# First attention batch from unsplit float32 operands, and new call orders on all five queues

## What is computed

```python
q  = (layernorm(x) @ w_q)           # 16 heads of 64, w_q 256 x 1024
kv = context @ w_kv                 # context 8 x 120 x 256, w_kv 256 x 2048
x  = x + tanh(g0) * (softmax(q k / 8) v @ w_out + b_out)
z  = layernorm(x)
gate = top-2 of softmax(z @ Wr.T), renormalised      # 8 experts
x  = x + tanh(g1) * sum_e gate_e * (silu(z @ W1_e.T) @ W2_e.T)   # DFF 1024
```

## Time and profile before

| what | us |
|---|---|
| median of 3 runs | 570.75 |
| lowest and highest of the 3 | 564.15, 574.33 |
| the profiled execution | 573.52 |
| its span in the profile | 571.5 |

### The profile page before, as it was taken

One profiled execution on the slowest core, in us unless ns is written; L12 is line 12 of the kernel. 1 busy time (PEld: TensorE's weight loads), 2 busy tenths in 40 slices (PEclk: granted clock), 3 DMA queues, 4 the chain that ended last, 5 costly groups with the idle time before them and its releaser, 6 DMA issues.

```text
span 571.5 us, 17675 instructions
## 1 busy us (share of the span) xinstructions
PE 484.5 (85%) x6526; PEld 428.0 (75%) x6527; DVE 361.5 (63%) x855; ACT 370.4 (65%) x576; POOL 365.6 (64%) x372
## 2 busy tenths in 40 slices
PE   0268799999999999997969799893999999999990
PEld 0156668888888888884859688783898898988980
DVE  4988897988988888989845456431343434444430
ACT  1877999998989898998533655351555555555540
POOL 0796977798989898999984372224355455444531
PEclk9998999999999999999776989996999999999996
DMA  8921514262725344342298569664678776878421
GB/s 275 395 81 51 191 59 165 74 223 39 248 52 177 114 131 147 111 161 47 95 136 326 136 98 292 196 199 108 197 213 240 222 239 199 255 206 261 111 32 16
DMA packets 34846, 93.13 MB, mean 163 GB/s; under 512 B 4967, under 2 KB 24565, under 8 KB 27490
## 3 DMA queue, kind: packets, MB, share of 16 engines
q1 hardware_dynamic: 25634, 81.86, 44.8%
q0 software_dynamic: 8576, 10.30, 9.6%
q10 hardware_dynamic: 576, 0.14, 0.1%
HBM read 74.17 MB, written 18.12 MB: 161 GB/s over the span
## 4 chain that ended last, share of the span: by engine, by line
DMA 36%; PE 20%; POOL 15%; issue 10%; DVE 10%; ACT 6%; POOLq 0%; SPq 0%; ACTq 0%; DVEq 0%
DMA out<-yt,row_of 34%; PE j_bank L1719 6%; POOL stage L632 5%; PE j_bank L1614 4%; POOL pT L587 4%; POOL stage L634 2%; ACT pT L834 2%; PE st_bank L1794 2%; ACT pT L833 2%; DMA w2s<-in_ctxT 2%; POOL w2s L636 2%; PE o_bank L1614 2%; PE j_bank L1681 2%; PE max_pair L1773 1%; PE st_bank L1614 1%
## 5 line engine op out<-in xcount | busy, mean ns | idle before, releaser
L681 POOL DMA_INDIRECT out<-yt,row_of x39 | 65.8, 1688 | 121.8 <-DMA out<-yt,row_of 108.0
L1614 PE MATMUL st_bank<-xsT,w_tile 128*128 128x128 f16 x1872 | 115.8, 223 | 4.0 <-issue 3.7
L1614 PEld LDWEIGHTS st_bank<-xsT,w_tile 128*128 128x128 f16 x1872 | 111.2, 100 | 6.3 <-issue 5.0
L1453 DVE SCALAR_TENSOR_TENSOR hT<-hf,h_scale,hT 128x512 f16<-128x512 f32 x78 | 58.3, 751 | 90.5 <-ACT hT L961 90.4
L1614 PE MATMUL o_bank<-w2s,hT 128*128 x936 | 110.2, 275 | 1.5 <-DVE yt L1462 0.8
L1614 PEld LDWEIGHTS o_bank<-w2s,hT 128*128 128x128 f16 x936 | 90.6, 99 | 12.6 <-issue 2.0
L955 ACT ACTIVATE hf<-st_bank,z_scale 128x512 f32<-128x512 f32 x78 | 52.9, 678 | 45.3 <-PE st_bank L1614 43.0
L587 POOL TENSOR_TENSOR pT<-pT 120x512 f16<-120x512 f32 x64 | 76.3, 1206 | 4.4 <-ACT pT L834 4.2
L961 ACT ACTIVATE hT<-hf,h_scale 128x512 f16<-128x512 f32 x78 | 56.3, 722 | 14.3 <-PE o_bank L1614 5.8
L833 ACT ACTIVATE pT<-st_bank,exp_bias,logit_scale 120x512 f32<-120x512 f32 x64 | 50.0, 781 | 12.8 <-PE st_bank L1797 9.2
L632 POOL TENSOR_SCALAR stage<-stage,upw 128x512 f32<-128x512 f32 x32 | 54.0, 1688 | 5.1 <-ACT w_hi L928 4.7
(11 more groups left out here) (208 smaller groups left out, 908.4 us busy)
## 6 DMA issues: line engine op xcount, KB each, us to landing
w_tile<-w_split SPq DMA_DIRECT2D x39, 1024.0 KB, 5.2
stage<-in_w SPq DMA_DIRECT2D x16, 1024.0 KB, 5.2
w_split<-w_hi SPq DMA_DIRECT2D x8, 512.0 KB, 2.9
w_split<-stage SPq DMA_DIRECT2D x8, 512.0 KB, 4.0
out<-x SPq DMA_DIRECT2D x17, 128.0 KB
w2s<-in_wkv SPq DMA_DIRECT2D x2, 1024.0 KB, 10.2
xin<-in_x SPq DMA_DIRECT2D x8, 256.0 KB, 3.2
xres<-in_x SPq DMA_DIRECT2D x16, 128.0 KB
```

Source lines behind the costliest of these rows:

```text
L681: pool.indirect_dma_start(out=out[0:rows], out_offset=bass.IndirectOffsetOnAxis(row_of[:, t:t + 1], 0), in_=yt[t % XG][:], in_offset=None, ...
L1453: nc.vector.scalar_tensor_tensor(out=hT[par][:, 1, 4 * a:4 * a + 4, :], in0=hf[par][:, 512 * a:512 * a + 512].rearrange("p (c n) -> p c n" ...
L1614: ins = pe.matmul(out, lhs[i](a), rhs[i](c), start=(i == 0 and a + c == 0), stop=(i == n - 1 and a == 1))
```

## The change

1. Batch 0's keys, queries and values are computed from unsplit float32 operands, in one plain float32 matmul per pair of blocks instead of three float16 ones. The scale factors are multiplied into the other operand (`first_context` on DVE, twice; `x_low(0)`), so the results come out in the same scale. `x_high(0)` goes. The float32 copies lie in `xn2` and `xn2T`, unused at that time.
2. The context's piece for batch 0 goes. The splits of the weights are moved behind batch 0's products in the call orders, and on POOL and in `split_high` they wait until these products are done. `SUMS` changes from (2, 4) to (1, 3).
3. SP loads x of batch 0 first, then w_q, context, w_k, w_v, four x tiles, w_out, and then x of batch 1 (which waits for `x_T(0)`) ahead of the stage loads.
4. New call orders on all five queues and in the four job lists. No instruction is added or removed by this part. In them, on PE, `tile_T(0)`, `tile_T(1)` and three up halves stand ahead of `values(7, 3, 0)`; before it was `tile_T(0)` and one up half. On DVE `tile_experts(4, 0)` stands right behind `norm2_rows(5)`; before it was behind `route(5)` and more. On POOL `gather(5)` stands ahead of `norm2_factors(7)`; before it was behind it. `gather(13)` stands behind `add(8)` in both.

```diff
-SUMS = (2, 4,)
+SUMS = (1, 3,)
-PIECES = (((0, M), (M, B * M)), ((0, INNER // 2), (INNER // 2, INNER)), ...
+PIECES = (((M, B * M),), ((0, INNER // 2), (INNER // 2, INNER)), ...
...
+            sp.dma_start(xin[:], x_b[0]).then_inc(xin_in, 16)
+            sp.dma_start(raw_q, wq).then_inc(raw_in[2], 16)
+            sp.dma_start(raw_ctx, ctxT).then_inc(raw_in[0], 16)
+            sp.dma_start(raw_k, wkv[:, :, 0:INNER]).then_inc(raw_in[1], 16)
+            sp.dma_start(raw_v, wkv[:, :, INNER:2 * INNER]).then_inc(raw_in[3], 16)
...
+            load_x(1)
...
                 pool.wait_ge(w_high[i][j], 1)
+                for name in {1: ("K" + "ab"[j],), 2: (f"Q{2 * j}", f"Q{2 * j + 1}"), 3: ("V" + "ab"[j],)}.get(i, ()):
+                    pool.wait_ge(job_full, JOBS.fulled(name, 0))
...
+            def first_context(b, i):
+                if b:
+                    return
+                w = (1, 3)[i]
+                dve.wait_ge(up_done[0], 1)
+                dve.wait_ge(up_done[w], 1 + (i > 0))
+                nc.vector.tensor_scalar(ctx32[i], raw_ctx[:, :, 0:M], up[:, 0:1], up[:, w:w + 1], ALU.mult,
+                                        ALU.mult).then_inc(ctx32_done, 1)
...
+                if b == 0:
+                    src = bank_full("XT", b)
+                    dve.wait_ge(up_done[2], 1)
+                    nc.vector.tensor_scalar(xnT32, src[:], up[:, 2:3], None, ALU.mult).then_inc(job_free, 1)
+                    return
...
+            def plain(out, lhs, rhs):
+                for i in range(len(lhs)):
+                    ins = pe.matmul(out, lhs[i], rhs[i], start=(i == 0), stop=(i == len(lhs) - 1))
+                return ins
...
+                    if b == 0:
+                        ins = plain(dst[:, q * N:(q + 1) * N], [raw_q[:, kc, c * P:(c + 1) * P] for kc in range(KC)],
+                                    [xnT32[:, kc * N:(kc + 1) * N] for kc in range(KC)])
+                        continue
```

More of the change, by code:

```diff
@@ L119, in positions @@
     @staticmethod
-    def positions(order):
+    def positions(order, without=None):
         at = {}
@@ new lines, in _ @@
+            sp.dma_start(raw_o, wo).then_inc(raw_in[4], 16)
+            load_x(1)
+            sp.dma_start(stage[0][:], w12_v[0][0]).then_inc(stage_in[0], 16)
+            sp.dma_start(stage[1][:], w12_v[1][0]).then_inc(stage_in[1], 16)
+            sp.dma_start(x_rest[1], x_v[:, RESTS[1][0]:sum(RESTS[1]), :]).then_inc(x_all_in[1], 16)
+            sp.wait_ge(spare_zero, 1)
+            sp.dma_start(out[T:T + P, :], x2[1][:]).then_inc(x2_out[1], 16)
+            for i in range(2):
+                sp.dma_start(xn2_dram[T + 64 * i:T + 64 * i + 64, :], x2[1][64 * i:64 * i + 64, :]).then_inc(xn2_out[i], 16)
@@ new lines, in _ @@
+                split_low(p + 7, 1, 2)
+                tile_add(p, 7)
+                split_low(p + 7, 1, 3)
+                p_low(p + 7, 1, 0)
+                tile_gather(p + 6, 4)
+                p_low(p + 7, 1, 1)
+                tile_add(p + 1, 6)
+                tile_add(p - 3, 8)
+                norm_factors(p + 8, 1)
+                tile_gather(p + 5, 6)
+                tile_gather(p + 5, 7)
+                tile_gather(p + 7, 0)
+                tile_gather(p + 4, 10)
+                weight_low(p + 8, 0, 0)
@@ new lines, in _ @@
+                score_scale(p + 2)
+                norm_o(p, 2, 0)
+                row_max(p + 1, 2)
+                tile_low(p, 1)
+                norm_o(p, 2, 1)
+                tile_gated(p - 3, 2)
+                split_low(p + 1, 0, 0)
+                o_low(p, 1, 0)
+                tile_gated(p - 24, 8)
+                tile_gated(p - 1, 0)
+                attn_scales(p + 3, 2)
+                v_low(p + 1, 0)
+                tile_h_low(p, 0, 0)
+                norm_o(p, 3, 0)
+                q_low(p + 2, 0)
@@ new lines, in _ @@
+                tile_low(p - 1, 3)
+                tile_h_low(p - 1, 2, 0)
+                split_low(p + 1, 0, 2)
+                tile_gated(p - 23, 7)
+                q_low(p + 2, 3)
+                weight_max(p + 2, 4)
+                tile_low(p - 21, 9)
+                x_stats(p + 1, 2)
+                norm2_rows(p - 1)
+                count_tiles(p - 2, 0, 2)
+                tile_low(p - 9, 7)
+                tile_experts(p - 2, 0)
+                tile_h_low(p - 21, 7, 0)
+                weight_low(p, 3, 1)
@@ new lines, in _ @@
+                tile_h_low(p - 22, 8, 1)
+                constants(p + 3)
+                norm_o(p + 1, 0, 0)
+                split_low(p + 1, 1, 1)
+                tile_h_low(p - 1, 2, 1)
+                tile_h_low(p - 21, 7, 1)
+                tile_h_low(p - 24, 9, 1)
+                tile_h_low(p - 7, 5, 1)
+                tile_gates(p - 23, 1)
+                tile_low(p - 25, 10)
+                o_low(p, 1, 1)
+                row_ids(p - 2, 0)
+                attn_scales(p + 2, 3)
@@ new lines, in _ @@
+                tile_T(p, 4)
+                values(p + 1, 2, 0)
+                weight_maxima(p + 2)
+                tile_up(p + 1, 0, 0)
+                o_T(p + 1, 1, 0)
+                tile_down(p - 34, 7)
+                v_product(p + 2, 0)
+                tile_up(p + 1, 0, 1)
+                tile_down(p - 12, 4)
+                tile_up(p - 34, 9, 1)
+                tile_up(p - 9, 5, 1)
+                values(p + 1, 2, 1)
+                tile_up(p + 1, 1, 0)
+                q_product(p + 3, 0)
@@ L1964, in _ @@
                 col_scores(p + 2, 0)
-                tile_up(p, 2, 0)
-                values(p + 1, 3, 0)
-                v_product(p + 2, 1)
-                logits(p)
             pe.wait_ge(experts_done, 2)
```

629 lines of the change are left out of this document (287 added, 342 removed).

## The result

The changed kernel took 562.33 us (median of 20 runs, 559.19 to 566.33), the kernel before 570.29 beside it (20 runs). The ratio is 0.9887, 95% interval [0.9865, 0.9908]: 6.4 us faster by the ratio, 8.0 by the medians. That is clear of the scatter and inside 2%. The changed kernel was timed three more times, on two chips, as a control of the experiments: 0.9921 [0.9883, 0.9958], 0.9897 [0.9856, 0.9938] and 0.9897 [0.9857, 0.9936]. The ratios leave out executions in the slower state (over 1.5% above the fastest of the same kernel), so a ratio can differ from the quotient of the medians: in the first control the medians, 570.51 and 571.11, lie only 0.1% apart.

The account below looks back on a forecast made before the run. POOL's work was taken to set the steady batch's 31 us, PE nearly level and bounding the tile loop. 573.5 - 7.5 - 3.7 - 3.7 + 1.0 = 559.6, or 557 on the median's scale; range 546 to 569.

Parts of the forecast that it names:

- the start (-7.5): Batch 0: POOL's first `split_low` starts at 40.4 instead of 47.94, 7.5 us earlier; ends 5.4 and 9.7 us.
- the first w1 tile (-3.7): Hand-over to the tiles: the load lands ahead of PE's first up half, so its 3.7 us wait goes.
- gather 5 (-3.7): Tile loop: issued ahead of `norm2_factors(7)`, gather 5 is early and PE's second 3.7 us wait goes.
- the wait of 9.4 us for gather 13: PE at tile 13: wait left in at no gain, as gather 13 stays behind add 8; ends -11.8 and +4.
- all three stalls go: Rival, tile loop: adds start earlier, the chain keeps up and gather 13 is in time, 545 us; chance 0.12.
- wait that takes the place of the one removed: Rival "only the start counts": PE reaches the tiles earlier but meets the same waits, 564 us; chance 0.25.
- The float32 products: Batch 0's queries, keys and values on PE: taken at 0, ends -2.4 to +3.4 us against 10.5 in float16.
- the sign of being wrong that I had named, over 14 us: Batch 0 on PE: float32 products taking over 14 us would show the forecast wrong.
- DVE held by POOL: Start: short DVE steps such as `first_context` slowed beside POOL's long ones; +1.0 us, at worst 4.5.
- ACT's list sets the pace: Start: ACT's 21.2 us of work from 17.0 to the first `split_high` paces it, taking 25.5 us at its busy share.
- The start is eaten: Rival, first two batches: DVE, not ACT, paces them, so POOL gains little, 570 us; chance 0.10.
- The steady rounds: Steady attention batches: POOL's 28.6 us of work stay, so no gain; -3 to +4 us over six batches.

Follow-up runs that it names:

- adds_out: Kernel before without the adds of expert tiles 0 to 3, whose rows are missing from the output: 561.86 us, ratio 0.9823.
- down0_late: Changed kernel with tile 0's down product behind tile 4's transposes and its DVE gate behind tile 2's first half: 563.26 us, ratio 0.9931.
- gather13_before: Kernel before with gather 13 issued ahead of add 7 instead of behind add 8: 569.15 us, ratio 1.0032.
- down0_first: Kernel before with tile 0's down product and its gate on DVE ahead of tile 1's up products: 576.02 us, ratio 1.0020.
- pool_waits: Changed kernel, but POOL's low part of the context starts only after DVE's scale steps for w_v and w_out: 570.38 us, ratio 0.9972.
- gathers_ahead_before: Kernel before with every gather from 13 on issued two adds earlier: 569.19 us, ratio 0.9981.
- handover_back: Changed kernel with the first w1 load put back behind batch 5's norm store and gather 5 behind norm2_factors(7): 567.24 us, ratio 0.9926.
- gather9_first: Changed kernel with gather 9 issued ahead of add 3 instead of behind it: 568.32 us, ratio 0.9953.
- start_alone: Changed kernel's start up to the first split of expert 0, then the call orders of the kernel before: 575.44 us, ratio 1.0087.
- the fourth set: Runs sharing a chip; its three of the changed order: unaltered 0.9897, gather 13 ahead of add 7 0.9863, tile 0's down product later 0.9931.
- before: The kernel before the change, unaltered: 570.29 us beside the changed kernel's first timing.
- after_fourth: The changed kernel unaltered, timed again as the control of the fourth set: 560.72 us, ratio 0.9897.
- after_third: The changed kernel unaltered, timed again as the control of the third set: 568.84 us, ratio 0.9897; its profiled execution took 576.3 us.

## Why the prediction was wrong

*The step that failed.* The sum was made of three gains: the start (-7.5), the first w1 tile (-3.7) and gather 5 (-3.7). In the profiles they are worth 0.7 us together when expert 7 is split and 0.6 when PE comes to tile 10. The term that I put at 0, the wait of 9.4 us for gather 13, gave 9.1 us of waiting (9.38 to 0.26), and 9.7 us of the 11.8 between the profiles stand at tile 13. The forecast said: "The order gather 13 behind add 8 stays, so I let the 9.4 us stay". The order stays, but add 8 itself is 13.2 us earlier, and the wait goes. So the mechanism was that of the rival "all three stalls go", to which I gave a chance of 0.12. That the range holds the result is luck: gains that did not come and one that I had left out offset each other.

`adds_out` shows in the kernel before, by the adds alone, what the wait is worth (0.9823). `down0_late` points the same way in the changed kernel (the wait back with 4.3 us, the median 2.5 us higher), but its interval does not stand clear. My argument against, that the slow transfer stays, was right as to the transfer (12.68 us for add 1 before, 11.56 for add 2 after) and wrong as to the chain: it starts at 318.19, not at 328.00. From tile 0's transposes to add 0 it is 27.4 us, not 39.5. DVE's gate of tile 0, before and after, and add 0 of the kernel before:

```profile
321.86 0.47 DVE L1462 TENSOR_SCALAR yt<-o_bank,gate_y 128x256 f32<-128x256 f32 x1
...
316.07 0.48 DVE L1489 TENSOR_SCALAR yt<-o_bank,gate_y 128x256 f32<-128x256 f32 x1
...
328.00 1.64 POOL L681 DMA_INDIRECT out<-yt,row_of  x1 [7.47 <-issue]
```

So 5.8 of the 9.8 us lie ahead of the gate and 4.0 behind it, where POOL of the kernel before stands idle for a reason that its profile does not name. I took the first part to be the moved calls (tile 0's and tile 1's up halves and tile 0's down product stand earlier in the orders of PE, ACT and DVE together). That is not shown, and there is a rival: the kernel before has its w1 wait and the lower clock (0.51) just there. `gather13_before` has the order of before with a wait of 1.54 us there instead of 3.74 and the full clock from 304 us on (0.50 from 304 to 308 in the kernel before), and its gate ends at 317.65, though its add 0 still goes out only at 325.61. `down0_first` shows that the one product alone doesn't do it. Nor does the start fix the rest: `pool_waits` has add 0 at 327.11 and add 8 at 385.63, `down0_first` 324.61 and 395.29.

*What sets the end.* Each add waits for the landing of the one before, and in the 20 profiles of this study the span ends 177.0 to 180.6 us behind the issue of add 8: 392.49 + 179.0 before, 379.32 + 180.4 after. That alone does not make the adds the cause, since from tile 13 on PE works through at 5.7 us a tile as well. In 19 of the profiles the last add goes out 4.3 to 5.1 us behind the start of PE's last product. The span ends 171.6 to 172.4 us behind tile 13's transposes in the twelve where PE waits at most 0.4 us for a gather there and for none behind, and 173.8 to 174.9 in the six with a wait of 4.3 to 9.4 us at tile 13. What the adds decide is how late PE gets through tiles 13 and 14. Take PE's wait away with the adds as late as before, and they come last themselves: in `gathers_ahead_before` an add goes out 9.4 us behind its tile's gate at tile 13, 9.2 at tile 30 and 6.4 at tile 38 (3.8, 3.7 and 1.5 in the kernel before). A late chain makes up next to nothing in the loop. This says why moving gathers won nothing: PE was late for gathers that were late for adds, and the two gather moves in the kernel before only changed which of the two was seen waiting.

*The first w1 tile (-3.7) and gather 5 (-3.7).* Both waits went, as forecast, and neither reached the total. PE came to tile 10 at 374.43 instead of 375.02, since 8.92 us for gather 9 took their place. `handover_back` (gather 5 late again) cost nothing, and `gather9_first` won nothing; the w1 term has no run of its own. The "wait that takes the place of the one removed" was the rival that I had only for the whole, not for these two terms.

*The start (-7.5).* Measured -3.1, for two reasons. (1) The float32 products, which I took at 0 with +3.4 as the end, cost about +5 at the full clock's rate and +7 as they ran. The program issues 16 query products of 256 columns and the trace records two instructions for each: (1.99 - 0.27)/7 = 0.246 us a record at the full clock, 0.49 a matmul, beside 0.11 for float16; the 16 key products took 3.73 us; two of the four value products 1.93 at the full clock. That is 7.9 + 3.7 + 3.9 = 15.5 us, beside 10.5 in float16 by my estimate. As they ran it was 8.21 + 1.99 + 3.73 + 3.56 + 1.93 = 19.4 us, beside 12.4 for the same products in the kernel before. So the sign of being wrong that I had named, over 14 us, was met. The first 24 records took 0.35 us each although the granted clock of their stretch reads 1.00; why stays open. ACT waits 3.0 us for the products. The rule that I had put aside, in the Trainium skill ("FP8 and Floating Point Precision", section "TensorE Precision Notes"), four passes for true FP32, agrees: 4.4 times a float16 matmul for the queries, and 4.3 for the keys (0.223 us beside 0.051). (2) DVE held by POOL, which I took at +1.0 with an end of 4.5: 5.24 us for scale steps that take 1.45 alone, so +3.8, paid by way of `x_T(1)` as 5.60 us of ACT. The low part of w_k's half paid too, 2.95 us for 1.28, a term that the sum did not have. "ACT's list sets the pace" was right, but the list has 9.0 us of waits in it. What the Trainium skill states ("GPSIMD Engine Reference", section 1), that GpSimd shares its SBUF interfaces with VectorE, agrees with these numbers.

*The 3.1 us don't last.* At expert 1's split they are gone: the moved weight splits lie in the second round, which `start_alone` makes likely and no run isolates. "The start is eaten" had a chance of 0.10 and was what happened to this part.

*The steady rounds (0, from -3 to +4).* The changed order takes 30.8 to 31.0 us a round in four profiles (the first one and the three of the fourth set) and 31.3 to 31.7 in nine others, beside 31.1 to 31.4 for the order of before (31.6 in `start_alone`, behind the changed start): between -2 and +4 us over six rounds, inside the ends. The nine are those in which PE and ACT stand together, all from three chips; in the four, the first profile and three from one further chip, it does not happen once. As far as thirteen profiles can tell it goes by the chip, not by the run. What makes the two engines stand stays open; moving the load of x did not move it.

*Right:* the first product near 17 us, the period within its bound, the hand-over's two waits gone, a wait of 9 us for a gather (at tile 9, not 13). *Not right among the signs:* the first split at 38 to 43 (44.86), and no wait of PE above 2 us from 280 to 330: at 293.86 it waits 2.40 for DVE, for attention's values just ahead of its first up half.

Open: what starts the chain earlier, a moved call or the stall and the clock, and whether an add chain that isn't serial would give the 10 us to either kernel. It wasn't tried, since two adds can meet in a row of the output.

## What to carry to other kernels

When an engine waits for a transfer, follow the issue back until something is reached that waits for nothing but its own kind; here gathers 9, 13 and 14 took turns at being waited for, all of them issued behind one serial chain of adds. Test such a chain by leaving its first links out before moving its neighbours: one run told what three moved gathers did not. And before calling a stage bound by one such chain, look whether another engine keeps the same pace beside it. Cost a changed number format by its own rate, or give it its full upper end, where the trace has only another kind of operation to go by.

## What the runs showed of the hardware

- A float32 matmul with 256 moving columns takes 0.49 us at the full clock, recorded as two instructions of 0.246; float16 takes 0.11. Float32 transposes of 128 columns, recorded once each, take 0.13.
- A DVE instruction of 128 x 2 takes 0.17 us alone and 2.42 beside a POOL instruction with two large operands, and ends with it; one of 128 x 240 goes from 0.39 to 3.14, and one of 128 x 1024 from 1.28 to 2.95.
- An indirect add into rows of the output lands after 3.7 to 4.1 us at the end of the run (`before`, adds 34 to 37), after 4.3 to 5.9 beside the loads of W1 in the loop (adds 13 to 32), and after 11.6 to 13.9 behind four indirect scatters (11.56 in the first profile, 13.94 in `after_fourth`); with the scatters moved away it was 3.88.
- On three chips ACT of one order of calls stands for 1.7 to 2.2 us in each of four rounds (3.0 once), with PE held beside it; on another chip it never does.
- In `after_third` a stall of PE of 2.8 us, followed by a granted clock of 0.59, goes with 6 more us of lateness at tile 2 and with a wait that is back 90 us later.
